# Gated cross-attention and expert layer, one core: order of the narrow matmuls and turning of the row maxima

## The reference

```python
def _L0_xattn_ref(x, cross_input, ...):          # x is layernormed
    att = einsum('bhqd,bhkd->bhqk', q, k) * scale  # 16 heads of 16, 512 x 512, causal
    y = einsum('bhqk,bhkd->bhqd', softmax(att), v)
    attc = einsum('bhqd,bhkd->bhqk', qc, kc) * scale   # 512 x 64
    y = y + einsum('bhqk,bhkd->bhqd', softmax(attc), vc)
    return y @ Wp + bp
x = x + tanh(g_xattn) * xattn(layernorm(x), ctx)
x = x + tanh(g_ffn) * ffn(layernorm(x))          # 15 experts, top 2 of 16, and a shared gated part
```

## Time and profile before

| what | value |
|---|---|
| median of three executions | 1625.32 us |
| span of the profiled execution | 1623.5 us |
| TensorE matmuls busy | 1532.1 us, 94% |
| VectorE busy | 1214.7 us, 75% |
| ScalarE busy | 882.0 us, 54% |
| GpSimd busy | 886.2 us, 55% |
| share of TensorE in the chain that ended last | 79% |
| share of VectorE in it | 11% |
| mean granted TensorE clock | 0.983 |

### The profile page before, as it was taken

The page is one execution under the profiler, slowest core; times in us unless marked ns, Lnnn a source line. Parts: engine busy times, 40 slices in busy tenths (PEclk is TensorE's granted clock), DMA queues, the critical chain, the costliest instruction groups (busy, mean ns, idle before and its releaser), DMA issues.

```text
span 1623.5 us, 36170 instructions
## 1 busy us (share of the span) xinstructions
PE 1532.1 (94%) x11348; PEld 941.6 (58%) x11411; DVE 1214.7 (75%) x3093; ACT 882.0 (54%) x1823; POOL 886.2 (55%) x1529
## 2 busy tenths in 40 slices
PE   4899999999999999999999999999997999999696
PEld 2445555555555555555555555555544789998564
DVE  4777787878787777878787877778855566775797
ACT  3365565656655655656566655556460344443555
POOL 2244455564646465555646464655645456776663
PEclk8999999999999999999999999999998999999999
DMA  6754445445454545454454545454464587654897
GB/s 162 197 135 128 140 145 148 147 129 172 137 163 142 151 145 148 133 148 148 143 170 143 144 143 160 139 150 131 142 208 159 161 254 229 176 164 147 262 315 251
DMA packets 185750, 268.32 MB, mean 165 GB/s; under 512 B 26648, under 2 KB 131360, under 8 KB 185568
## 3 DMA queue, kind: packets, MB, share of 16 engines
q1 hardware_dynamic: 149344, 196.34, 43.1%
q0 software_dynamic: 12960, 36.51, 6.1%
q10 hardware_dynamic: 23264, 33.19, 6.0%
HBM read 160.28 MB, written 105.66 MB: 164 GB/s over the span
## 4 chain that ended last, share of the span: by engine, by line
PE 79%; DVE 11%; DMA 3%; ACT 3%; issue 2%; SPq 1%; POOL 1%; DVEq 0%; ACTq 0%; POOLq 0%
PE pv_self L1431 10%; PE scalar_bank L1368 10%; PE scalar_bank L1357 10%; PE vector_bank L1405 7%; PE vector_bank L1901 7%; PE pv_cross L1414 4%; PE vector_bank L1314 4%; PE vector_bank L1402 4%; DVE nmax L1199 4%; PE vector_bank L1474 3%; PE vector_bank L1347 3%; PE vector_bank L1398 2%; PE vector_bank L1447 2%; PE scalar_bank L1888 2%; PE pv_cross L1909 2%
## 5 line engine op out<-in xcount | busy, mean ns | idle before, releaser
L1199 DVE TENSOR_REDUCE nmax<-vector_bank 128x1 f32<-128x384 f32 (+4 forms) x832 | 513.9, 640 | 108.1 <-PE vector_bank L1405 106.7
L869 ACT ACTIVATE pt<-scalar_bank 128x512 f32<-128x512 f32 x640 | 363.4, 598 | 239.7 <-PE scalar_bank L1368 238.0
L700 POOL TENSOR_SCALAR_AFFINE_SELECT pt<-pt 128x256 f32<-128x256 f32 (+1 forms) x640 | 228.0, 367 | 269.1 <-ACT pt L869 262.3
L1368 PE MATMUL scalar_bank<-stack 99*64 99x512 bf16 (+4 forms) x1280 | 294.1, 321 | 1.9 <-DMA stack<-max_scratch 1.0
L1405 PE MATMUL vector_bank<-stack 96*128 96x128 bf16 (+3 forms) x1024 | 248.3, 301 | 3.4
L1357 PE MATMUL scalar_bank<-xnT,w_qk 128*128 128x512 f32 x384 | 182.6, 599 | 1.1 <-ACT xnT L794 1.1
L1735 POOL DMA_INDIRECT rows<-pt x142 | 138.4, 975 | 80.0 <-issue 62.6
L1431 PE MATMUL pv_self<-pt,vst 128*32 128x512 f32 (+3 forms) x2048 | 181.0, 442 | 0.0
L1402 PEld LDWEIGHTS vector_bank<-tri,ident_b 128*128 128x128 bf16 x704 | 68.2, 97 | 190.9 <-DVE nmax L1199 110.3
L1402 PE MATMUL vector_bank<-tri,ident_b 128*128 128x128 bf16 (+2 forms) x641 | 151.8, 237 | 16.1 <-DMA stack<-qk_scratch 10.8
L659 POOL DMA_INDIRECT rows<-xn,slot x128 | 134.1, 1047 | 52.1 <-issue 28.8
(11 more groups left out here) (304 smaller groups left out, 2676.3 us busy)
## 6 DMA issues: line engine op xcount, KB each, us to landing
qk_scratch<-parts SPq DMA_DIRECT2D x31, 1200.0 KB, 4.6
stack<-qk_scratch SPq DMA_DIRECT2D x120, 192.0 KB, 3.0
pt<-rows SPq DMA_DIRECT2D x142, 132.0 KB, 2.4
stack<-qk_scratch SPq DMA_DIRECT2D x248, 72.0 KB, 2.6
pt<-rows SPq DMA_DIRECT2D x16, 1024.0 KB, 6.3
stack<-qk_scratch SPq DMA_DIRECT2D x124, 128.0 KB, 3.1
stack<-qk_scratch SPq DMA_DIRECT2D x240, 36.0 KB, 2.2
xt<-in_x_dram ACTq DMA_DIRECT2D x15, 512.0 KB, 3.9
```

The lines of the kernel that those rows point to most:

```text
L700: pool.affine_select(out=v, in_=v, compare_op=ALU.is_ge, fill=0.0, base=0, pattern=pat, channel_multiplier=-1).then_inc(masked, 1)
L869: act.activation(dst, bank(kind, ("st", c, k))[:, :], ACT.Exp, scale=SCALE).then_inc(scalar_drained, 1)
L1199: dve.tensor_reduce(dst, src, axis=AX, op=ALU.max, negate=True).then_inc(vector_drained, 1)
L1368: return pe.matmul(out, stack[c][0:rows, head, key0:key0 + nk], stack[c][0:rows, head, q0:q0 + nq], start=True, stop=True, **kw)
```

## The change

The attention's TensorE program gets a function `narrow_products`. The two cross score units of a group are made one after the other at slots 0 and 12, and the cross values that are due in that stretch follow them at once: at slot 12 those of group 0 of the same half, at slot 0 of half 1 those of group 1 of half 0. Slots 1 and 13 have no score of their own left, only their work beside. Self values go by two key tiles: after slots 16 and 20 instead of 16, 18, 20, 22, and in half 1 after slots 3 and 7 instead of 1, 3, 5, 7. After the loop of half 1 the turning of the cross sums of group 0 comes ahead of the cross values of group 1, which then stand directly in front of the self values.

The maxima are kept with the query tile as the last index, so that the 3 parts, 8 rows of heads and 4 query tiles are 96 consecutive columns. They are turned by one transpose of 96 columns, copied as 96 partitions by 128, and stored to the same places in HBM as 96 rows of 256 bytes instead of 24 of 1024. The load is unchanged.

```diff
--- before.py
+++ after.py
@@ -254,9 +254,9 @@
         vst = sb("vst", [P, QT, KC, HU, 32])
         vcst = sb("vcst", [P, KC, HU // 2, 64])
         nmax = [sb(f"nmax{c}", [P, QT, HU, 2]) for c in range(KC)]
-        mres = sb("mres", [P, QT, HU])
-        mparts = [sb(f"mparts{g}", [P, QT, 3, HU], BF16) for g in range(2)]
-        mT = [[sb(f"mT{c}{g}", [3 * HU, T], BF16) for g in range(2)] for c in range(KC)]
+        mres = sb("mres", [P, HU, QT])
+        mparts = [sb(f"mparts{g}", [P, 3, HU, QT], BF16) for g in range(2)]
+        mT = [[sb(f"mT{c}{g}", [3 * HU * QT, P], BF16) for g in range(2)] for c in range(KC)]
         pt = [sb(f"pt{g}", [P, 10, 512]) for g in range(2)]
         ct_all = sb("ct", [P, 2, 2, 512])
         ct = [ct_all[:, g, :, :] for g in range(2)]
@@ -466,7 +466,7 @@
 
                 heads = slice(HEAD_GROUP * g, HEAD_GROUP * (g + 1))
                 sp.wait_ge(vector_drained, VU.upto(kind, b, ("mT", c, g)))
-                sp.dma_start(mscr[c, g].rearrange("s (h t) -> (s h) t", t=T), mT[c][g][:, :]).then_inc(m_stored, 16)
+                sp.dma_start(mscr[c, g].rearrange("s (n t) -> (s n) t", t=P), mT[c][g][:, :]).then_inc(m_stored, 16)
                 sp.wait_ge(m_stored, 16 * MSPLIT.upto(kind, b, (c, g)))
                 sp.dma_start(stack[c][STACK:STACK + MROWS, heads, 0:K0],
                              mscr[c, g].rearrange("s (h t) -> s h t", h=HEAD_GROUP)).then_inc(m_in[c][g], 16)
@@ -670,8 +670,8 @@
                 elif g == 0 and PARTS[kind][1]:
                     pool.wait_ge(vector_filled, VU.upto(kind, b, ("mT", 1, 1)))
                 pool.sem_inc(passed, 1)
-                src = nmax[c][:, :, HEAD_GROUP * g:HEAD_GROUP * (g + 1), :].rearrange("p q h s -> p q (h s)")
-                h, m, l = (mparts[g][:, :, i, :] for i in range(3))
+                src = nmax[c][:, :, HEAD_GROUP * g:HEAD_GROUP * (g + 1), :].rearrange("p q h s -> p (h s) q")
+                h, m, l = (mparts[g][:, i, :, :] for i in range(3))
                 pool.tensor_copy(h, src).then_inc(msplit_step, 1)
                 pool.wait_ge(msplit_step, 3 * n - 2)
                 pool.tensor_tensor(mres[:, :, :], src, h, ALU.subtract).then_inc(msplit_step, 1)
@@ -1200,7 +1200,7 @@
 
             def max_transposed(kind, b, c, g):
                 ps = filled(kind, b, ("mT", c, g))
-                dve.tensor_copy(mT[c][g][:, :], ps[:, :].bitcast(BF16)[0:3 * HU, 0:T]).then_inc(vector_drained, 1)
+                dve.tensor_copy(mT[c][g][:, :], ps[:, :].bitcast(BF16)[0:3 * HU * QT, 0:P]).then_inc(vector_drained, 1)
 
             def normalise(kind, b, c, g, w):
 
@@ -1323,10 +1323,8 @@
                 ps = claim_v(kind, b, ("mT", c, g))
                 pe.wait_ge(msplit_done, MSPLIT.upto(kind, b, (c, g)))
                 pe.sem_inc(passed, 1)
-                for q in range(QT):
-                    last = pe.transpose(ps[:, :].bitcast(BF16)[0:3 * HU, q * P:(q + 1) * P],
-                                        mparts[g][:, q, :, :].rearrange("p s h -> p (s h)"), ident_b[:, :])
-                last.then_inc(vector_filled, 1)
+                pe.transpose(ps[:, :].bitcast(BF16)[0:3 * HU * QT, 0:P],
+                             mparts[g][:, :, :, :].rearrange("p s n q -> p (s n q)"), ident_b[:, :]).then_inc(vector_filled, 1)
 
             def transpose_inputs(kind, b):
                 pe.wait_ge(xn_ready, LN.upto(kind, b, 0))
@@ -1511,6 +1509,27 @@
                 if (c, k) == (1, 13):
                     combine.hole_gate(pe, 1)
 
+            def narrow_products(kind, b, c, k):
+
+                start = k % len(GROUP)
+                if k == len(GROUP):
+                    pe.wait_ge(m_in[c][1], 16 * (b + 1))
+                if start == 0:
+                    score_unit(kind, b, c, k)
+                    score_unit(kind, b, c, k + 1)
+                    if k > 0:
+                        pv_cross_products(kind, b, c, 0)
+                    elif c == 1:
+                        pv_cross_products(kind, b, 0, 1)
+                elif start > 1:
+                    score_unit(kind, b, c, k)
+                if k in (16, 20):
+                    for kt in KT_ORDER[(k - 16) // 2:(k - 12) // 2]:
+                        pv_self_products(kind, b, c, 0, kt)
+                if c == 1 and k in (3, 7):
+                    for kt in KT_ORDER[(k - 3) // 2:(k + 1) // 2]:
+                        pv_self_products(kind, b, 0, 1, kt)
+
             def main(kind, b, c):
                 prev, cur, nxt = PARTS[kind]
                 if cur:
@@ -1518,25 +1537,14 @@
                     pe.wait_ge(vector_drained, VU.start(kind, b))
                 for k in range(NST):
                     if cur:
-                        if k == len(GROUP):
-                            pe.wait_ge(m_in[c][1], 16 * (b + 1))
-                        score_unit(kind, b, c, k)
-                        if c == 1 and k == 0:
-                            pv_cross_products(kind, b, 0, 1)
-                        if c == 1 and k in (1, 3, 5, 7):
-                            pv_self_products(kind, b, 0, 1, KT_ORDER[(k - 1) // 2])
-                        if k == 14:
-                            pv_cross_products(kind, b, c, 0)
-                        if k in (16, 18, 20, 22):
-                            pv_self_products(kind, b, c, 0, KT_ORDER[(k - 16) // 2])
+                        narrow_products(kind, b, c, k)
                     beside(kind, b, c, k)
                     if kind == "post":
                         shared_units(c, k)
                 if cur:
+                    transpose_sums(kind, b, c, 0, "x")
                     if c == 1:
                         pv_cross_products(kind, b, 1, 1)
-                    transpose_sums(kind, b, c, 0, "x")
-                    if c == 1:
                         for kt in KT_ORDER:
                             pv_self_products(kind, b, 1, 1, kt)
                     if c == 1 or not nxt:
```

## The result

| | before | after |
|---|---|---|
| median | 1624.38 us (4 runs) | 1580.51 us (4 runs, 1578.51 to 1582.69) |
| ratio | | 0.9731, 95% interval 0.9718 to 0.9744 |
| span of the profiled execution | 1623.5 us | 1576.8 us |
| one repeating batch | 74.05 us | 70.97 us |

The change is 2.7% faster. Forecast were 1578 us and a span of 1576.5.

What follows compares the result with a forecast made beforehand. TensorE, with matmuls in flight for 94% of the span, bounds the kernel. It loses 3.86 us of work a batch, 3.0 kept: 48 in 16, less 1, 47; span 1576.5, median 1578 us, range 1562 to 1602.

Steps and rivals of the forecast that it cites:

- price of a visit: On TensorE, each stretch of narrow work (weights of 64 columns or fewer) costs 0.09 us entering, 0.12 leaving, beside its streams.
- fourth rival: On TensorE, the visit's price only moves; only the transposes' streams go, 11 us, part lost: 1619 us; chance 0.04.
- price of the fp32 weight loads: On TensorE, the visit's price might really belong to these loads, all still there; the prediction would then fail as a whole.
- 96 columns count as wide: Turning of the maxima on TensorE: no visit paid, 0.36 us saved each; bounds 0.17 and 0.36.
- What VectorE takes back: Vector banks freed late hold TensorE up: of 3.86 us less work in a batch, 3.0 reach the end.
- second rival: Narrow blocks starve VectorE, which bounds the attention loops; TensorE waits for banks: 1605 or 1596 us; chance 0.15.
- C: Half 1, slots 0 to 11: 0.84 us less TensorE work in a batch, 0.55 kept after a wait for VectorE's bank.
- D: Half 1, slot 12 to batch end: 1.27 us less work, 1.25 kept; VectorE's arrears worked off behind the loop.
- copy of the turned maxima: Behind the turning: 0.40 us for 512 elements, taken at 0.2 with 128 elements; bounds 0.1 and 0.4.
- last batch: End of the attention: 1 us less gain, since no projections follow and it already waits for other things there.
- store of maxima: Store to HBM with 256-byte rows: taken as unchanged, 0.7 us spare; bounds 0.5 us shorter to 2 us longer.
- third rival: Small rows make the store late at slot 12, half 0; slower overall if 3.7 us longer; chance 0.04.

Runs made afterwards that it cites:

- The two narrow transposes: The changed kernel with the maxima turned by two transposes of 64 and 32 columns instead of one of 96; 1638.17 us, ratio 0.9804 to the kernel before.

## Why the prediction was right

- **The price of a visit** (0.09 in, 0.12 out) was the step on which all rested. The merged groups came out at 1.64 and 0.79 us against 1.66 and 0.81, and two cross scores with the cross values at 1.42 (571.78 to 573.20) against 1.47, so an exit fewer is worth 0.14 us there and the price was a little low. The two narrow transposes brought the visit back. The fourth rival (the price only moves) is out, and so is a price of the fp32 weight loads, which are all still there.
- **96 columns count as wide**: the row at 576.90 has neither 0.09 ahead nor 0.1 behind. I took the upper bound and it was the value. The page "TensorE: Matmul & The Clock Gate" of the Trainium skill, section "LDWEIGHTS", by which its weight load would be slower, has the right direction: the trace after gives 122 ns where 24 columns took 92 and 128 columns 99. It shows in no start to start.
- **What VectorE takes back** was 0.78 us of 3.86 in a batch, forecast 0.84. The 3.86 is the forecast's own sum and not a reading; what the trace shows is that TensorE's listed waits for VectorE's reductions grew from 1.0 to 1.5 us in the two batches above, under the 1 us more that was to speak for the second rival. The sum is better than its terms. C was sized at 0.55 and kept 0.32: the wait at the turning was foreseen at 0.8 and is 0.61, but its neighbours had less to give back. D was sized at 1.25 and kept 1.52, more than the 1.27 of work that left: there I had left out the wait of 0.5 us in the kernel before, at the routing's ranks, which the earlier cross values now cover. The argument that was given for D failed at its other end: VectorE's arrears were to be worked off behind the loop, but the turning of the cross sums claims a vector bank and the change puts it ahead of those values, where it waits 0.54 us (615.64 above; before, at 713.74, it did not wait). Two misses of about 0.5 us with opposite signs make D look near; that much of the close sum is luck. I had looked for waits that the new order adds and not for those that it ends.
- **The copy of the turned maxima** takes 0.21 us (taken at 0.2), against 0.40 in the earlier trace rows.
- **The last batch** gained 4.1 us (56.2 to 52.1) in the two profiles, 1 more than the others where 1 less was forecast. The clock made the difference. In this batch the kernel before has a stretch at the lower level (a window over 1193.6 to 1197.0 shows a granted clock of 0.50), and the kernel after has none (its next begins at 1177.7, the batch ends at 1169.4). Without some 1.7 us for that stretch (an estimate from the repeating batches) the gain is about 2.4, 0.7 less than in the others, as was forecast. When the kernel after ran again, its last batch had 6.9 us at the lower level and took 54.6 us. The batches from the first end to the last sum to a gain of 43.7 us with the clock's 3.3 us counted against it.
- **The clock** was no term of the sum. It cost 3.3 us in the repeating batches of the profiled execution and gave back 1.7 in the last, where the kernel before had lost them. That the forecast span is met within 0.3 us is luck; the forecast is right to two or three, as the median shows (1578 against 1580.5).
- **The store of maxima**: in the waits of SyncE, the load of maxima stood 101.5 us behind the store before and 129.6 after, 64 times each, 1.6 against 2.0 us. So the store with rows of 256 bytes took 0.4 us more on the mean; it had been taken as unchanged. That is inside the spare time which I read from the earlier trace rows, and the cross scores of slot 12 show no wait. The rule of the page "DMA: Bandwidth & Descriptors" of the Trainium skill, section "Specifications", on rows under 512 bytes has the right sign here. The third rival's point of decision, 3.7 us, was far off.

Two rows of the forecast's list came true literally: 11 entries into narrow work in a batch instead of 27, and batches at 71.0 us.

## What to carry to other kernels

Where an engine is at 94% busy, compare start to start with the streaming of the columns, by pairs of neighbours: about 0.1 us at every change of weight width is, for 27 visits, 5.7 of the 74.05 us of a batch (an estimate, 27 x 0.21), and no share of busy time shows it. The change took 16 of the 27 away. Merging such visits pays as long as the work that is left between them does not run into the other engines. Here blocks of two key tiles (1.64 us) pay. With four in a block (2.3 us) the gain was lost, by waits at the place that the narrow work had left and by the clock. Of a moved piece of work ask both ways: which wait it uncovers where it left, and which it covers where it now stands.

## What the runs showed of the hardware

A weight load of 24, 32 or 64 columns behind a matmul with 128, and the reverse, was not made ahead of its matmul by more than 0.03 us, and the change cost 0.09 us going in and 0.10 to 0.14 coming out. A load of 96 columns was made ahead, like one of 128.

In the repeating batches with self values in pairs, the granted clock fell to the lower level for 3.4 us at a time while TensorE was busy without a gap, behind matmuls that stream 64 and 16 columns each. It did so in some batches and not in others that run the same instructions in the same order (2 of 14 in the kernel after, 1 of 14 when it ran again), at a cost of 1.7 us each. That the place of the second pair matters is supported by the tally over 14 profiles; how the chip decides was not tested.
